# Attention one's prologue re-ordered: which stacks load first, statistics by two tiles, one subtraction on VectorE, 22 gathers moved

## The reference

```python
h = W.T[tokens]                                                  # token embedding
h = h + attn1(layernorm(h))    # 16 heads of 16, scores masked by 0, then softmax
h = h + moe(layernorm(h))      # 4 experts, the best 2 of them
h = h + attn2(layernorm(h))    # relative positions, softmax over the batch axis
h = h + ffn(layernorm(h))      # blockwise FP4 quantisation, SiLU gate
# attn1:
qkv = einsum('bhce,ef->bhcf', xh, Wqkv) + bqkv                   # the same 16x48 for all heads
att = softmax((q @ k.T / 4) * tril(ones, k=-1))                  # masked scores count as 0
out = (att @ v).reshape(b, c, d) @ Wr + br
```

## Time and profile before

| | us |
|---|---|
| three runs | 2956.3, 2959.09, 2963.05 |
| median | 2959.09 |
| the profiled execution | 2954.28 |
| its span | 2952.5 |
| PE busy in the span | 2543.3 (86%) |
| DVE busy | 2114.0 (72%) |
| ACT busy | 1509.7 (51%) |
| POOL busy | 1644.1 (56%) |

### The profile page before, as it was taken

The page is one execution under the profiler, slowest core; times in us unless marked ns, Lnnn a source line. Parts: engine busy times, 40 slices in busy tenths (PEclk is TensorE's granted clock), DMA queues, the critical chain, the costliest instruction groups (busy, mean ns, idle before and its releaser), DMA issues. The chain is left out here.

```text
span 2952.5 us, 58168 instructions
## 1 busy us (share of the span) xinstructions
PE 2543.3 (86%) x15254; PEld 1489.2 (50%) x15318; DVE 2114.0 (72%) x5668; ACT 1509.7 (51%) x3246; POOL 1644.1 (56%) x2564
## 2 busy tenths in 40 slices
PE   1768888888888888888876999999999979999999
PEld 0323433333443333443354666666666647666676
DVE  2656667766666776766646999999999865565554
ACT  1335555555555555555532655565555544444444
POOL 3663343433343433343244878888877757776775
PEclk7679999999999999999977999999999979999999
DMA  3343433443443443443340000000000000000000
GB/s 57 92 111 58 64 57 51 64 71 51 64 60 54 57 72 54 61 64 52 58 139 0 1 1 0 0 0 0 0 0 0 1 4 17 14 16 14 16 16 18
DMA packets 81255, 112.93 MB, mean 38 GB/s; under 512 B 25101, under 2 KB 37145, under 8 KB 80537
## 3 DMA queue, kind: packets, MB, share of 16 engines
q1 hardware_dynamic: 76360, 101.44, 20.1%
q0 software_dynamic: 3072, 8.39, 1.0%
q10 hardware_dynamic: 1744, 2.16, 0.2%
HBM read 18.98 MB, written 8.39 MB: 9 GB/s over the span
## 5 line engine op out<-in xcount | busy, mean ns | idle before, releaser
L661 DVE TENSOR_REDUCE cand<-ring 128x4 f32<-128x512 f32 x1152 | 713.5, 681 | 389.4 <-PE ring L771 369.8
L570 ACT ACTIVATE probs<-scoresT 128x512 f32<-128x512 f32 x1152 | 624.4, 605 | 624.9 <-PE scoresT L715 622.3
L491 POOL TENSOR_SCALAR_AFFINE_SELECT probs<-probs 128x256 f32<-128x256 f32 x512 | 204.8, 414 | 464.9 <-ACT probs L570 458.2
L715 PE MATMUL scoresT<-stage 98*128 98x512 bf16 (+3 forms) x1536 | 381.6, 340 | 41.8 <-ACT probs L570 28.0
L735 PE MATMUL pv<-probs,Vg 128*32 128x512 f32 (+3 forms) x3072 | 344.6, 573 | 23.8 <-POOL probs L491 18.0
L771 PE MATMUL ring<-Km,Qm 64*128 64x512 bf16 (+2 forms) x1792 | 230.3, 323 | 95.8 <-DVE cand L661 44.5
L1198 PE MATMUL mm<-w_W,hT 128*128 128x256 f32 x1024 | 243.2, 381 | 8.0 <-ACT z L1286 3.3
L1218 PE MATMUL mm<-w_W,x2T 128*128 128x512 f32 x512 | 242.7, 597 | 0.3 <-DVE x L1437 0.2
L715 PEld LDWEIGHTS scoresT<-stage 98*128 98x128 bf16 x1536 | 122.1, 99 | 219.3 <-ACT probs L570 126.6
L771 PEld LDWEIGHTS ring<-Km,Qm 64*128 64x128 bf16 x1792 | 76.5, 96 | 295.7 <-issue 120.1
L1279 ACT ACTIVATE hT<-mmT,w_be,w_g 128x128 f32<-128x128 f32 x512 | 185.5, 468 | 78.1 <-PE mmT L1209 78.1
(11 more groups left out here) (254 smaller groups left out, 5270.0 us busy)
## 6 DMA issues: line engine op xcount, KB each, us to landing
stage<-parts SPq DMA_DIRECT2D x256, 96.0 KB, 2.8
stage<-parts SPq DMA_DIRECT2D x256, 64.0 KB, 2.8
Qm<-parts SPq DMA_DIRECT2D x128, 128.0 KB, 2.6
Km<-parts SPq DMA_DIRECT2D x128, 128.0 KB, 2.7
stage<-parts SPq DMA_DIRECT2D x256, 32.0 KB, 2.4
out<-result SPq DMA_DIRECT2D x64, 128.0 KB, 1.7
stage<-ct SPq DMA_DIRECT2D x128, 4.0 KB
w_W<-in_W SPq DMA_DIRECT2D x4, 512.0 KB
```

What stands on the lines that cost most here:

```text
L491: nc.gpsimd.affine_select(out=d, in_=d, compare_op=ALU.is_gt, fill=0.0, base=0, pattern=[[0, 2], [1, P]], channel_multiplier=-1).then_inc( ...
L570: nc.scalar.activation(probs[:, buffer(slot), :], scoresT[slot % SCORE_BANKS][:], ACT.Exp, scale=SOFT).then_inc(exp_ok, 1)
L661: ins = nc.vector.tensor_reduce(c, src[:].rearrange("p (t a b) -> p t a b", t=c.shape[1], b=P), AX.X, ALU.max)
L715: ins = nc.tensor.matmul(scoresT[slot % SCORE_BANKS][:, at:at + hi - lo], Ks[0:ROWS, gi, hh, P * kt:P * kt + P], Qs[0:ROWS, gi, hh, lo:hi] ...
```

## The change

- `ALONE`, `LN_LATER`, `window`: the statistics for half batch 1 stand at place 3 (right behind XT) instead of 13, their LN_POWER at 14. MID_LAG is 2, V stands at 10. The maxima's steps of the prologue stand at every other place. Three GATHER events are new in the prologue: 4 gathers behind the first LN_POWER, 10 behind the second, 8 before the tenth of the 18 maxima's steps. LOAD_FIRST stands before LOAD.
- LOAD_FIRST is one event: the four `Qm` loads after `parts_ok` 2, the four `Km` loads after 4.
- `gat0` is one semaphore per two tiles; each pair of statistics waits for its own pair of gathers. `gat1` counts the gathers of batch 1 alone, `gat2` the rest; the latter is waited for from section `loop` on.
- The remaining 34 gathers stand at the even slots of section `first`.
- In the prologue the last subtraction (MID) is VectorE's.
- SyncE issues `b_v` after all of `gat0`, then `ident2`, `future2` and, last, `w_r`. TensorE's and VectorE's waits at their start are gone: TensorE waits for `w_in` (now 16 loads) before the projections, for `late_in`, `const_ok` and `minus_ok` before the first maxima; VectorE for `bv_in` and `const_ok` before the sum with `b_v`.
- Attention one's semaphores are cleared and freed at its end, with one more barrier of all engines.

```diff
-LN_LATER = 13
+LN_LATER = 3
+
+
+GATHERED = (0, 4, 14, 22)
...
-ALONE = {"LN_STATS": (0, 0, 0, 0), "LN_NORM": (1, 1, 1, 1), "XT": (2, 2), "QK": (8, 9, 10, 11), "MID_LAG": 1, "V": 12, "PV_COPY": 1, "TMP": 2, "PT": 5, "OT": 11,
+ALONE = {"LN_STATS": (0, 0, 0, 0), "LN_NORM": (1, 1, 1, 1), "XT": (2, 2), "QK": (8, 9, 10, 11), "MID_LAG": 2, "V": 10, "PV_COPY": 1, "TMP": 2, "PT": 5, "OT": 11,
...
-        at(pos_of["LN_STATS"][-1] + (0 if scores else LN_LATER * (ahead - 1)), ("LN_POWER", ahead))
+        at(pos_of["LN_STATS"][-1] if scores or ahead == 1 else pos_of["LOAD"], ("LN_POWER", ahead))
...
         at(pos_of["VG"], ("VG",))
+        if not scores:
+            at(pos_of["LN_NORM"][0], ("GATHER", 0))
+            at(pos_of["LOAD"], ("GATHER", 1), ("LOAD_FIRST",))
+            at(pos_of["MX"] + MAX_BANKS * 2, ("GATHER", 2))
         at(pos_of["LOAD"], ("LOAD",))
-        if not scores:
-            at(pos_of["LOAD"], *(("LOAD_FIRST", p) for p in range(PAIRS_MX)))
...
-            at(MAX_AT[n // 2] if scores else pos_of["MX"] + n, *u)
+            at(MAX_AT[n // 2] if scores else pos_of["MX"] + 2 * n, *u)
...
+                for s in gat0:
+                    sp.wait_ge(s, 16 * LN_TILES)
                 sp.dma_start(b_v[:].rearrange("p (a b) -> p a b", a=8),
-                             dram["bqkv"][None, None, 32:48].broadcast_to([P, 8, 16])).then_inc(w_in, 16)
-                sp.dma_start(w_r[:], dram["Wr"].rearrange("(c p) n -> p c n", p=P)).then_inc(w_in, 16)
+                             dram["bqkv"][None, None, 32:48].broadcast_to([P, 8, 16])).then_inc(bv_in, 16)
...
+                        elif e[1] == "LOAD_FIRST":
+                            sp.wait_ge(parts_ok, 2)
+                            for p in range(PAIRS_MX):
+                                rows = slice(32 * p, 32 * p + 32)
+                                for i in range(2):
+                                    sp.dma_start(Qm[i:P:2, p, :], parts[rows, 0, i:i + 1, :].broadcast_to([32, 2, S])).then_inc(max_in[p], 16)
+                            sp.wait_ge(parts_ok, 4)
+                            for p in range(PAIRS_MX):
+                                rows = slice(32 * p, 32 * p + 32)
+                                for i in range(2):
+                                    sp.dma_start(Km[i:P:2, p, :], parts[rows, 1, 0:2, :]).then_inc(max_in[p], 16)
...
+                def gather_other(n):
+                    gather(TPB + n, gat1 if n < TPB else gat2)
+
                 for t in range(TPB):
-                    gather(t, gat0)
+                    gather(t, gat0[t // LN_TILES])
...
-                            if section == "first" and gi * UNITS + slot < TILES - TPB:
-                                gather(TPB + gi * UNITS + slot, gat1)
+                            n = GATHERED[-1] + (gi * UNITS + slot) // 2
+                            if section == "first" and slot % 2 == 0 and n < TILES - TPB:
+                                gather_other(n)
...
-                                dve.wait_ge(gat0, 16 * TPB)
+                                dve.wait_ge(gat0[e[3]], 16 * LN_TILES)
                             elif section == "first":
-                                dve.wait_ge(gat1, 16 * (TILES - TPB))
+                                dve.wait_ge(gat1, 16 * TPB)
+                            elif e[3] == 0:
+                                dve.wait_ge(gat2, 16 * (TILES - 2 * TPB))
...
+                        elif kind == "MID" and section == "init":
+                            w, c = e[2:4]
+                            dve.wait_ge(mid_ok, 2 * w + c + 1)
+                            nc.vector.tensor_tensor(parts[:, w, 2, 512 * c:512 * c + 512], f32part[:, c, :],
+                                                    parts[:, w, 1, 512 * c:512 * c + 512], ALU.subtract).then_inc(parts_ok, 1)
...
+        nc.clear_and_free_semaphores(sems)
+        nc.all_engine_barrier()
```

More of the change, by code:

```diff
@@ L258, in sb @@
             return ctx.enter_context(nc.sbuf_tensor(name, shape, dt))
+        sems = []
         def sem(name):
-            return ctx.enter_context(nc.semaphore(name))
+            sems.append(nc.alloc_semaphore(name=name))
+            return sems[-1]
         w_qkv = sb("w_qkv", [P, 3, P])
@@ L312, in attention_one @@
         tok_in, w_in, const_ok, pool_c = sem("tok_in"), sem("w_in"), sem("const_ok"), sem("pool_c")
-        gat0, gat1 = sem("gat0"), sem("gat1")
+        gat0, gat1, gat2 = [sem(f"gat0_{n}") for n in range(LN_PARTS)], sem("gat1"), sem("gat2")
+        bv_in, late_in = sem("bv_in"), sem("late_in")
         filled, read_dve, read_act = sem("ring_filled"), sem("ring_read_dve"), sem("ring_read_act")
@@ L388, in _ @@
                         rows, half = slice(HALF * j, HALF * j + HALF), slice(HALF * i, HALF * i + HALF)
-                        sp.dma_start(ident2[rows, i, :], ident_b[half, :]).then_inc(w_in, 16)
-                        sp.dma_start(future2[rows, i, :], future[half, :]).then_inc(w_in, 16)
+                        sp.dma_start(ident2[rows, i, :], ident_b[half, :]).then_inc(late_in, 16)
+                        sp.dma_start(future2[rows, i, :], future[half, :]).then_inc(late_in, 16)
+                sp.dma_start(w_r[:], dram["Wr"].rearrange("(c p) n -> p c n", p=P)).then_inc(late_in, 16)
                 def run(section, hb, it):
@@ L415, in run @@
                                 put(Ks, hh, 80, 1, parts[rows, 1, 2:3, :], k_in)
[L416 to L424, removed]
+                        elif e[1] == "LOAD_FIRST":
[9 more added lines that the diff above has]
+                                    sp.dma_start(Km[i:P:2, p, :], parts[rows, 1, 0:2, :]).then_inc(max_in[p], 16)
+                        elif e[1] == "LOAD_MAX":
+                            p = e[2]
+                            last = [x for x in plans[section] if x[0] == e[0] and x[1:3] == ("R", "MX")
+                                    and x[4:6] == (2 * p + 1, MAX_BANKS - 1)][0]
+                            wait_apart(sp, (parts_ok, 4 * (hb + 2)), (filled, num(last[-1][0], 0) + 1))
+                            lo = 16 * (HPG * (1 - par) + 2 * p)
                             rows = slice(lo, lo + 32)
@@ L492, in run @@
                                                         pattern=[[0, 2], [1, P]], channel_multiplier=-1).then_inc(mask_ok, 1)
-                            if section == "first" and gi * UNITS + slot < TILES - TPB:
-                                gather(TPB + gi * UNITS + slot, gat1)
+                            n = GATHERED[-1] + (gi * UNITS + slot) // 2
+                            if section == "first" and slot % 2 == 0 and n < TILES - TPB:
+                                gather_other(n)
+                        elif kind == "GATHER":
+                            for n in range(GATHERED[e[2]], GATHERED[e[2] + 1]):
+                                gather_other(n)
                         elif kind == "LN_POWER":
@@ L505, in run @@
                                                     parts[:, w, 0, 512 * c:512 * c + 512], ALU.subtract).then_inc(rest_ok, 1)
-                        elif kind == "MID":
+                        elif kind == "MID" and section != "init":
                             w, c = e[2:4]
@@ L611, in _ @@
                 nc.vector.memset(Ks[STACK:P, :, :, :], -1.0).then_inc(minus_ok, 1)
-                dve.wait_ge(const_ok, 3)
                 def run(section, hb, it):
@@ L668, in run @@
                                     dve.wait_ge(rsum_ok, hb + 1)
+                                else:
+                                    dve.wait_ge(bv_in, 16)
+                                    dve.wait_ge(const_ok, 3)
                                 j = e[4]
@@ L743, in run @@
                             pair = e, [x for x in plans[section] if x[:4] == e[:4] and x[4:6] == (hh + 1, k)][0]
+                            if section == "init" and hh == k == 0:
+                                pe.wait_ge(late_in, 16 * LATE)
+                                pe.wait_ge(const_ok, 3)
+                                pe.wait_ge(minus_ok, 1)
                             if k == 0:
@@ L787, in run @@
                                 w, c = e[4:6]
+                                if section == "init":
+                                    pe.wait_ge(w_in, 16 * WEIGHTS)
                                 read(pe, section, num, use(section, "XT", c))
```

5 lines of the change are left out of this document (1 added, 4 removed).

## The result

| | before | after |
|---|---|---|
| median of the runs, us | 2959.7 (4 runs, 2956.3 to 2963.05) | 2914.26 (4 runs, 2914.17 to 2915.42) |
| the profiled execution, us | 2954.28 | 2915.42 |
| its span, us | 2952.5 | 2913.7 |

The ratio is 0.9847, 95% interval 0.9835 to 0.9859: 45 us faster. It was forecast at 2907, range 2896 to 2925. The time lies in it, 7 us on the slow side.

The account below looks back on a forecast made before the run. TensorE-bound except at the start, a one-engine-at-a-time chain, then two windows with GpSimd hardly resting. 30.5 + 20 - 1 = 49.5 us gained: 2904.8 from the profile, 2909.6 from the median, so 2907; range 2896 to 2925.

Parts of the forecast that it names:

- Statistics and b_v: Prologue's start: statistics by two tiles, b_v behind the gathers; LN_POWER ends at 20.0 instead of 31.98, 12 us gained.
- The parts: Prologue's projections: last subtraction on VectorE, partly waiting for GpSimd; half the parts ready at 32.4 us, all at 36.3.
- Stacks: Prologue: the maxima's stacks loaded first; with the steps before, maxima begin at 39.7 instead of 70.17, 30.5 us gained.
- The maxima take 25.5: Prologue's maxima, bound by VectorE's reductions, take 25.5 us, so first scores come at 65.2.
- GpSimd ends the prologue: Rival, chance 0.03: the prologue's 18 gathers, each as slow as its landing (2.8 us), delay the scores 24 us: 2931.
- Windows 0 and 1: Attention one's first two windows: 22 of 56 gathers gone, GpSimd freed; 20 us gained, range 10 to 26.
- The end: Attention one's end: clearing the semaphores and one more barrier cost 1 us, range 0 to 3.
- The clock: Rival, chance 0.05: TensorE's granted clock rises later in the denser start; three windows at the lower level give 2998.
- GpSimd stays the bound: Rival, chance 0.13: GpSimd still bounds windows 0 and 1, which gain 10 us: 2915 on the profile, 2920 on the median.

Follow-up runs that it names:

- chips 4 and 15: The changed kernel run again unchanged: 2901.04 us on chip 4, 2902.18 us on chip 15; the kernel before, beside it, 2953.19 and 2954.15.
- the control's: Profile of the changed kernel, run again unchanged on chip 15 beside further experiments; profiled run 2902.2 us, median 2902.18 us.
- The two kernels meant to part gathers from loads: Against the changed kernel: 18 prologue gathers back in the windows, 2921.03 and 2916.68 us; 24 score-stack loads before the maxima's 8, 2923.41 and 2918.56 us.

## Why the prediction held, and where it was off

- **Statistics and b_v** (12 us): right, and shown by undoing: 8.2 us of it are b_v's, 3.1 the pairs'. Some 0.6 remain; the slowest gather landed 11.9 us after issue before and 10.9 with b_v alone put back, and no run says what made that difference.
- **The parts** (VectorE's subtraction, with waiting): right. L678 took 1.00 and 1.23 beside L530, 0.69 alone, and all parts were ready at 36.1 (36.3). The Trainium skill, "SBUF — State Buffer", section "SBUF: two separate sides", says that of a VectorE instruction with two inputs in SBUF and a GpSimd one that reads SBUF the later waits for the whole of the first. The trace agrees: L678 ended 0.54 and 0.56 us after L530, wherever it had begun. With the subtraction on GpSimd the maxima begin 2.4 us later.
- **Stacks** (30.5 us at the maxima, with the two steps above): 30.45 and 30.76. One term of the working was incomplete: of the order of the loads I counted the 24 as moved, not that the Qm loads also leave early; undoing it costs 18.5 and not 15.4. The sum was right since it was made from the positions.
- **The maxima take 25.5**: right in the profiles of chips 4 and 15 (25.5), wrong in that of the result (33.65). This term is 8.1 of the 10.6 us that the profile lacks. No rival of mine named it; "GpSimd ends the prologue" isn't it, since the gathers of that profile took 0.95 each and the casts waited for VectorE.
- **Windows 0 and 1** (20, from a range of 10 to 26): 20.0 in the result's profile, 24.2 in the control's, where they come to 86.4, under the 88.5 of two later windows. The cause was right and the size too small: the exact 20.0 holds 3.7 us by which window 1 is longer than in the control, and nothing in my step stands for those. Both factors count: 18 gathers fewer 8.9 us, spacing 10.4.
- **The end** (1): 0.75, read from the profile and not tested by a run.
- **The clock** rose and did not fall: 0.86 over the two windows, 0.75 before.
- **The number.** That 2907 came within 7 us is in part luck. It was set between 2904.8, worked out from the profile, and 2909.6, worked out from the median, and lies between two timings of the kernel (2901 and 2915) of which I foresaw neither. The measured 2915 is also what the rival "GpSimd stays the bound" gives on the profile, but by chance: its windows gain 10 us and these gained 20.

**Open.** What stops the maxima in some groups of runs and not in others. The stop stands in both profiles kept of the nine executions near 2915 and in neither of the two kept of the six near 2901; for the others only the time speaks. It belongs to a step of the kernel, and it doesn't stand in the one profile of the kernel before, in which neither the score-stack loads nor the gathers ran beside the maxima. The DMA share around it in the two stretches of 4 us from 44 on is 0.82 and 0.77, and 0.78 to 0.82 and 0.74 on the chips without it, so the traffic's amount alone isn't the cause. The two kernels meant to part gathers from loads ran on chips without a stop; that they have no stop themselves says nothing. A further rival is untested: the recording of the trace, which has its holes just there, may cause or lengthen the stop. Every execution has a span and a clock on record, so none is known to have run unrecorded. A late fetch of instructions is not it: in all five profiles with the stop no packet of the instruction queues runs from 10 us before the stop to its end.

## What to carry to other kernels

A load in very many small pieces (here 1024 of 64 bytes, 10 us) is cheap only where nobody waits for a DMA issued close to it: put it behind the transfers that a chain depends on, and look at the landing times of the others to find it. Work threaded into the slots of a busy engine costs by its density: an empty slot between gathers gave 10.4 us, a little more than 18 gathers fewer (8.9). And order loads by who waits for them first, splitting them where half of their source is ready.

## What was unexpected of the hardware

- The same program had two timings, 13 us apart: near 2915 in nine executions and near 2901 in six on two chips, with a 5 us stop at one step in the profiles of the former only. With it went 3.1 us more in the maxima and 3.7 in window 1. A forecast from one profile carries that uncertainty, 0.5% of the time.
- Two gathers of 128 KB landed 10.8 to 10.9 us after issue beside a 64 KB load in 1024 pieces of 64 bytes; with the load behind them the last was there 2.8 us after issue. After the change the load held four other gathers in the same way (issued from 20.23 on, first packet at 27.18), unnoticed since nobody in the prologue waits for them.
